# Three float32r passes for k, v and the scores of a fused attention stage, with one buffer for x's halves and the rotation of k moved ahead

## The reference

```
q = rms_norm((x @ wq) as 16 heads of 128) * q_norm_w      k = rms_norm((x @ wk) as 4 heads) * k_norm_w
v = (x @ wv) as 4 heads                                    k_ctx, v_ctx: 64 context rows per batch
q = q * cos + rotate_half(q) * sin                         k likewise; k_ctx is not rotated
scores = q . [k_ctx, k] / sqrt(128) + causal mask          probs = softmax(scores)
out = (probs @ [v_ctx, v]) @ wo                            x = x + tanh(g) * out
```

## Time and profile before

| | us |
|---|---|
| median of 3 runs (range) | 2099.92 (2099.11 to 2105.03) |
| the profiled execution, its own time | 2102.94 |
| its span, first to last instruction | 2101.2 |
| first score of slot 0 / end of the stage's last product, from the span's start | 55.92 / 1154.9 |

### The profile page before, as it was taken

The page is one execution under the profiler, slowest core; times in us unless marked ns, Lnnn a source line. Parts: engine busy times, 40 slices in busy tenths (PEclk is TensorE's granted clock), DMA queues, the critical chain, the costliest instruction groups (busy, mean ns, idle before and its releaser), DMA issues. The chain is left out here.

```text
span 2101.2 us, 27108 instructions
## 1 busy us (share of the span) xinstructions
PE 1903.4 (91%) x9540; PEld 1345.5 (64%) x9540; DVE 1112.5 (53%) x2265; ACT 1043.9 (50%) x2245; POOL 962.2 (46%) x862
## 2 busy tenths in 40 slices
PE   6899999999999999999998899999999768849998
PEld 4566766666666666666665777768999546624443
DVE  3444543456455664456443548624434468747886
ACT  2455555544454445444443321115665266647775
POOL 3544554344544444444441100007888336537774
PEclk8999999999999999999999799999999979979999
DMA  7111111211112111111000410036889580000000
GB/s 232 42 47 47 46 32 43 61 29 47 32 32 66 47 47 33 31 46 47 7 0 7 153 51 21 21 123 175 237 242 255 121 191 1 1 0 16 21 21 26
DMA packets 114005, 141.67 MB, mean 67 GB/s; under 512 B 37440, under 2 KB 69184, under 8 KB 113680
## 3 DMA queue, kind: packets, MB, share of 16 engines
q1 hardware_dynamic: 106704, 123.16, 19.1%
q0 software_dynamic: 7168, 16.78, 3.8%
HBM read 105.31 MB, written 29.36 MB: 64 GB/s over the span
## 5 line engine op out<-in xcount | busy, mean ns | idle before, releaser
L680 POOL TENSOR_TENSOR a_xcl<-xT,a_xch 128x512 fp32r<-128x512 f32 x64 | 82.4, 1288 | 406.5 <-ACT a_xch L510 406.5
L832 PE MATMUL a_A<-a_pT,a_vf 128*128 128x512 f32 (+1 forms) x448 | 239.8, 617 | 1.4 <-ACT a_pT L526 1.2
L597 DVE TENSOR_REDUCE a_nmax<-a_S 128x1 f32<-128x192 f32 (+3 forms) x256 | 138.6, 553 | 183.6 <-PE a_S L781 183.5
L780 PE MATMUL a_S<-a_kT,a_qT 128*128 128x288 f32 (+3 forms) x640 | 213.7, 432 | 2.2 <-ACT a_pr_odd L516 2.2
L120 PE MATMUL a_A<-a_wlo,a_xch 128*128 128x512 f32 x256 | 152.4, 595 | 32.1 <-DVE a_qb L643 26.5
L516 ACT ACTIVATE a_pr_odd<-a_S,a_nmax 128x320 f32<-128x320 f32 (+1 forms) x128 | 81.1, 635 | 180.4 <-DVE a_nmax L597 179.2
L526 ACT ACTIVATE a_pT<-a_TR 128x512 f32<-128x512 f32 (+1 forms) x224 | 133.4, 596 | 57.9 <-PE a_TR L822 57.7
L780 PEld LDWEIGHTS a_S<-a_kT,a_qT 128*128 128x128 f32 x640 | 121.3, 192 | 55.8 <-issue 24.8
L516 ACT ACTIVATE a_pr_even<-a_S,a_nmax 128x192 f32<-128x192 f32 (+1 forms) x128 | 67.2, 527 | 162.1 <-DVE a_nmax L597 162.0
L801 PE MATMUL a_A<-a_wkv,xT 128*128 128x256 f32 x512 | 136.9, 391 | 5.9 <-DVE a_qT L593 5.9
L1427 POOL TENSOR_TENSOR e_wlo<-expert_raw,e_whi 128x1408 fp32r<-128x1408 f32 x32 | 102.5, 3224 | 67.8 <-ACT e_whi L1500 67.8
(11 more groups left out here) (372 smaller groups left out, 5073.4 us busy)
## 6 DMA issues: line engine op xcount, KB each, us to landing
a_pw<-in_L_ffn_w_dram SPq DMA_DIRECT2D x96, 256.0 KB, 2.8
expert_raw<-in_L_ffn_w_gate_dram SPq DMA_DIRECT2D x16, 704.0 KB
expert_raw<-in_L_ffn_w_up_dram SPq DMA_DIRECT2D x16, 704.0 KB
expert_raw<-in_L_ffn_w_down_dram SPq DMA_DIRECT2D x16, 512.0 KB
tern<-a_tern SPq DMA_DIRECT2D x48, 128.0 KB, 1.7
x_res<-in_x_dram SPq DMA_DIRECT2D x4, 1024.0 KB, 8.8
a_raw<-in_L_xattn_wq_dram SPq DMA_DIRECT2D x4, 1024.0 KB, 5.6
a_raw<-in_L_xattn_wo_dram SPq DMA_DIRECT2D x4, 1024.0 KB, 5.4
```

What stands on the lines that cost most here:

```text
L597: ve.tensor_reduce(nmax[:, s % 2, i:i + 1], pair(s, i), AX.X, ALU.max, negate=True).then_inc(s_max, 1)
L680: pool.tensor_tensor(xcl[:, t % 2], xT[:, :, tok(t)], xch[:, t % 2].bitcast(F32), ALU.subtract).then_inc(xlo_ready, 1)
L780: pe.matmul(bank[:, lo:hi], qT[:, t % 2, hq], kT[:, par(t), lo:hi], start=True, stop=hi < nk)
L832: last = pe.matmul(A[:, A_USE["V", t, 0][0]], vf[r, par(t), i], pT[r, i % 2], start=i == 0, stop=i == nkt - 1)
```

## The change

k and v, and the scores, go through `mm3`. For that q and k are kept as halves after the transposition (`qTh`, `qTl`, `kTh`, `kTl`): ACT copies the high part from the bank, and DVE subtracts it from the bank (new letters l0, l1), which releases the bank and lets S0 go. The q halves have one buffer. The context keys land in `kcs`, and ACT and DVE split them once a batch (y). wk and wv land in `pw` and are split into `wkvh`, `wkvl` by ACT and POOL (u) in slot 13 of a group (DVE at the start); two pieces of the ternary weights are fetched later for that (`HELD`). x's halves have one buffer, those of tile s+2 are made in slot s, and k0 now waits for them. `qb` has two buffers. DVE's rotation of k (v) stands ahead of the third head's maximum, and both ternary pieces stand between N2 and M3. The wo halves are made at the end of slot 1 of a group. In POOL's order for the third tile, x now stands behind q. The tables of cosines and sines are loaded once.

```diff
-                -2: "k0 k1 H0 q0 q1 q2 q3 H1",
-                -1: "k0 k1 G0 R K T q0 q1 q2 q3 G1",
-                0: "S0 W0 W1 S1 W2 W3 P0 k0 S2 R k1 P1 V0 q0 P2 V1 S3 P3 K V2 q1 T P4 V3 q2 V4 q3",
-                1: "S0 W0 W1 S1 W2 W3 P0 k0 S2 R k1 P1 V0 S3 K q0 T V1 q1 q2 q3",
-                2: "S0 W0 W1 S1 W2 W3 P0 k0 S2 R k1 P1 V0 q0 S3 P2 V1 K q1 T V2 q2 q3",
-                3: "S0 W0 W1 S1 W2 W3 P0 k0 S2 R k1 P1 V0 q0 P2 V1 S3 P3 K V2 q1 T V3 q2 q3"}
+                -2: "k0 k1 q0 q1 H0 q2 q3 H1",
+                -1: "G0 k0 k1 K T R q0 q1 q2 q3",
+                "first": "S0 S1 k0 k1 G1 S2 R q0 S3 q1 K T q2 q3",
+                0: "S0 W0 W1 S1 W2 W3 P0 k0 k1 S2 R P1 V0 q0 P2 V1 S3 P3 K V2 q1 T P4 V3 q2 V4 q3",
+                1: "S0 W0 W1 S1 W2 W3 P0 k0 k1 S2 R P1 V0 S3 K q0 T V1 q1 q2 q3",
+                2: "S0 W0 W1 S1 W2 W3 P0 k0 k1 S2 R P1 V0 q0 S3 P2 V1 K q1 T V2 q2 q3",
+                3: "S0 W0 W1 S1 W2 W3 P0 k0 k1 S2 R P1 V0 q0 P2 V1 S3 P3 K V2 q1 T V3 q2 q3"}
...
-                 1: "x e0 j0 e1 g0 j1 e2 v r g1 n j2 e3 k t o f",
-                 2: "w x e0 j0 e1 g0 j1 e2 v r g1 n j2 e3 g2 k t o f",
+                 1: "x e0 j0 e1 g0 j1 v u e2 r g1 n w j2 e3 k t o f",
+                 2: "w x e0 j0 e1 g0 j1 v y e2 r g1 n j2 e3 g2 k t o f",
...
-    DVE_SLOT = "M0 M1 N0 D X j0 M2 N1 v N2 j1 M3 N3 B E A"
+    DVE_SLOT = "M0 M1 N0 D X v M2 N1 N2 y j0 j1 M3 l0 N3 l1 B E A"
...
-    POOL_ORDER = {-3: "r0 r1 r2 r3 x c0", -2: "w c1 x r", -1: "x q r", 0: "w x q p0 p1 r", 1: "x q p0 p1 r", 2: "w x q p0 p1 r", 3: "x q p0 p1 r"}
+    POOL_ORDER = {-3: "r0 r1 r2 r3 x w c0", -2: "c1 r", -1: "q x r", "first": "x q p0 p1 r",
+                  0: "x q p0 p1 r", 1: "x q p0 u p1 w r", 2: "w q x p0 p1 r", 3: "x q p0 p1 r"}
...
-                    if name == "x" and live(s, 3):
-                        t = s + 3
+                    if name == "x" and (s == BEGIN or live(s, 2)):
+                        t = 0 if s == BEGIN else s + 2
                         until(pool, xhi_ready, tile, t, m)
-                        pool.tensor_tensor(xcl[:, t % 2], xT[:, :, tok(t)], xch[:, t % 2].bitcast(F32), ALU.subtract).then_inc(xlo_ready, 1)
+                        pool.tensor_tensor(xcl[:], xT[:, :, tok(t)], xch[:].bitcast(F32), ALU.subtract).then_inc(xlo_ready, 1)
...
+                    if name == "l" and live(s, 1):
+                        t = s + 1
+                        if i == 0:
+                            until(ve, kh_ready, tile, t, m)
+                            ve.tensor_tensor(kTl[:, par(t), key_cols(t)], TR[:, TR_USE["K", t, 0][0], 0:P],
+                                             kTh[:, par(t), key_cols(t)].bitcast(F32), ALU.subtract).then_inc(kl_ready, 1)
+                        else:
+                            until(ve, qh_ready, tile, t, m)
+                            ve.tensor_tensor(qTl[:], TR[:, TR_USE["T", t, 0][0]], qTh[:].bitcast(F32), ALU.subtract).then_inc(ql_ready, 1)
...
                         if i == 0:
-                            until(pe, qT_ready, tile, t, m)
-                            until(pe, kT_ready, tile, t, m)
+                            until(pe, ql_ready, tile, t, m)
+                            until(pe, kl_ready, tile, t, m)
...
-                            pe.matmul(bank[:, lo:hi], qT[:, t % 2, hq], kT[:, par(t), lo:hi], start=True, stop=hi < nk)
+                            mm3(pe, bank[:, lo:hi], qTh[:, hq], qTl[:, hq], kTh[:, par(t), lo:hi], kTl[:, par(t), lo:hi], True, hi < nk)
...
                         if i == 0:
                             bank_of_A("k", t, s, m)
-                            if t < PERIOD:
-                                pe.wait_ge(xT_ready, t + 1)
+                            until(pe, xlo_ready, tile, t, m)
                             if t % PERIOD == 0:
-                                until(pe, wkv_loaded, lambda v: 32 * (v // PERIOD + 1), t, m)
+                                pe.wait_ge(kvl_ready, t // PERIOD + 1)
...
-                            last = pe.matmul(bank, xT[:, k, tok(t)], wkv[:, k].rearrange("p a n -> p (a n)"), start=k == 0, stop=k == KD - 1)
+                            last = mm3(pe, bank, xch[:, k], xcl[:, k], wkvh[:, k], wkvl[:, k], k == 0, k == KD - 1)
```

More of the change, by code:

```diff
@@ L168, in steps @@
     def steps(order, s):
-        return [(word[0], int(word[1:] or 0)) for word in order[s if s < 0 else s % BT].split()]
+        return [(word[0], int(word[1:] or 0)) for word in order[s if s < 0 else s % BT if s > 0 else "first"].split()]
     def batch_next(s):
@@ L176, in row, with context @@
         return i if s == BEGIN else s + ahead if BT <= s + ahead < PERIOD else None
+    def context(s):
+        return 0 if s == -1 else batch_next(s) // BT if s % BT == 2 and live(batch_next(s), 0) else None
     def bank_order(firsts):
@@ L362, in load_piece, with fetch_piece @@
                 def load_piece(k):
+                    if k < 2 * PIECES and all(k - held not in (0, 1) for held in HELD.values()):
+                        fetch_piece(k)
+                def fetch_piece(k):
                     j, o = k % PIECES // FFN_PIECES, k % FFN_PIECES
-                    if k < 2 * PIECES:
-                        sp.dma_start(pw[:, k % 2], piece(j, o)).then_inc(piece_loaded[k % 2], 16)
+                    sp.dma_start(pw[:, k % 2], piece(j, o)).then_inc(piece_loaded[k % 2], 16)
                 def store_tern(n):
@@ L478, in do @@
                                        ACT.Copy).then_inc(xT_ready, 1)
+                    if name == "u" and (s == BEGIN or s % PERIOD == PERIOD - 3):
+                        t = 0 if s == BEGIN else s + 3
+                        if live(t, 0):
+                            act.wait_ge(wkv_loaded, 32 * (t // PERIOD + 1))
+                            until(act, kv_full, tile, t - 1, m)
+                            act.activation(wkvh[:], wkv.rearrange("p k a n -> p k (a n)"), ACT.Copy).then_inc(kvh_ready, 1)
                     if name == "c":
@@ L489, in do @@
                         act.activation(vc[:, i], A[:, A_USE["G", i, 0][0]], ACT.Copy).then_inc(cv_copied, 1)
-                    if name == "y":
+                    if name == "y" and context(s) is not None:
+                        n = context(s)
+                        act.wait_ge(ck_loaded, 16 * (n + 1))
+                        act.activation(kTh[:, n % 2, 0:T], kcs[:], ACT.Copy).then_inc(ch_ready, 1)
+                    if name == "m":
                         act.wait_ge(gates_loaded, 32)
                         act.activation(gates[:], graw[:].rearrange("p l s -> p (l s)"), ACT.Tanh).then_inc(gates_ready, 1)
-                    if name == "w" and s % PERIOD in (2, 14):
-                        part = 0 if s % PERIOD == 14 else 1
-                        t = s + (2, -2)[part]
+                    if name == "w" and (s == BEGIN or s % PERIOD in (1, PERIOD - 2)):
+                        part = 1 if s % PERIOD == 1 else 0
+                        t = 0 if s == BEGIN else s + (2, -1)[part]
                         if live(t, 0):
@@ L570, in do @@
                         ve.tensor_scalar(veps[:, u:u + 1], mv[:, u, 1:2], 1e-5, None, ALU.add).then_inc(x_var, 1)
+                    if name == "y" and context(s) is not None:
+                        n = context(s)
+                        ve.wait_ge(ch_ready, n + 1)
+                        ve.tensor_tensor(kTl[:, n % 2, 0:T], kcs[:], kTh[:, n % 2, 0:T].bitcast(F32), ALU.subtract).then_inc(cl_ready, 1)
+                    if name == "l" and live(s, 1):
[7 more added lines that the diff above has]
+                            ve.tensor_tensor(qTl[:], TR[:, TR_USE["T", t, 0][0]], qTh[:].bitcast(F32), ALU.subtract).then_inc(ql_ready, 1)
                     if name == "X" and row(s, 5, i) is not None:
@@ L725, in bank_of_TR @@
                     if before is not None:
-                        sem, count = {"P": (pT_ready, turn(before[2])), "T": (qT_ready, tile), "K": (kT_ready, tile),
+                        sem, count = {"P": (pT_ready, turn(before[2])), "T": (ql_ready, tile), "K": (kl_ready, tile),
                                       "Z": (ctx_copied, tile), "R": (xT_ready, tile), "H": (ck_copied, tile)}[before[0]]
```

136 lines of the change are left out of this document (80 added, 56 removed), and 9 rows, old and new, of the table ACT_ORDER.

## The result

| | before | after |
|---|---|---|
| median of the runs side by side | 2100.21 us (7 runs) | 2110.46 us (2107.69 to 2113.05 in 6) |
| ratio, 95% interval | | 1.0043 [1.0031, 1.0055] |
| the profiled execution: own time / span | 2102.94 / 2101.2 | 2110.13 / 2108.3 |
| from the span's start to the first product after the stage | 1154.9 | 1157.6 |
| from there to the end: stages that the change does not touch | 946.3 | 950.7 |

The account below looks back on a forecast made before the run. TensorE, busiest at 91%, was taken as the bound, with late answers from other engines and its clock. Credits of -104 and debits of +115 gave +11 on the median 2099.9, hence 2110 us, range 2084 to 2134.

Parts of the forecast that it names:

- rival B: Whole kernel: the terms cancel, with low-clock stretches and ternary waits both at the low side; 2100 us, chance 0.23.
- (2): Scores on TensorE: three float32r passes cost less than plain float32 for most widths, nothing at the narrowest; -25 us.
- (3): q0's waits for DVE's rotation of k go, as the rotation stands earlier and k1 is done sooner; -26 us.
- (5): Nine low-clock stretches of TensorE in slots 24 to 55 go along with the waits before them; -15 us.
- (6): Start: -10 us before slot 0 and +6 in it, the first context block coming before the tables; -4 us.
- (7): k0 waits for x's halves, which POOL makes behind q in third tiles and in the first group; +71 us.
- (8): Ternary second and third tiles: both DVE pieces ahead of M3 make TensorE wait 1.1 and 2.0 us; +19 us.
- (9): ACT makes the wo halves before e3 in slots 17, 33 and 49; +2 us (0 to 5).
- (10): New TensorE waits bring 15 low-clock stretches at 1.5 us each; +23 us (5 to 35).
- rival D: Narrow score passes of 192 columns run at the float32 rate, +42 us; 2150 us, chance 0.07.
- rival C: DVE and POOL block each other: moved ternary pieces meet POOL, twelve slots pay 0.9 us more; 2121 us, chance 0.15.
- Rival A: New waits don't lower the clock, so that +23 us shrinks to +3, below five low stretches; 2089 us, chance 0.22.

Follow-up runs that it names:

- e4: Changed kernel with k and v as one plain float32 product of the high halves instead of three float32r passes; 2131.12 us, ratio 1.0137 to the kernel before.
- e3: Changed kernel with the scores as one plain float32 product of the high halves instead of three float32r passes; 2122.58 us, ratio 1.0096 to the kernel before.
- e2: Kernel before with only k0 and k1 side by side, the rotation earlier, ternary pieces behind N2 and two `qb` buffers, no split halves; 2059.89 us.
- e5: e1 plus, before slot 0, x ahead of q on POOL and the context keys' halves ahead of q's sums on ACT and DVE; 2045.95 us.
- e1: Changed kernel with POOL making x's low halves before q's normalization in third tiles; 2054.57 us, ratio 0.9772 to the kernel before.
- e6: Changed kernel with x ahead of both the wq halves and q in the third tile, on ACT and POOL; 2044.83 us.
- e7: e1 plus the fourth head's maximum moved between the two ternary pieces on DVE; 2036.06 us, ratio 0.9692 to the kernel before.

## Why the prediction was right, and where it was not

The sign, the time (2110) and the mechanism of the largest debit were right. The sum inside the stage was not: +11 was forecast and +2.7 measured. That the median came out at +10.3 is luck for the larger part: 4.4 us lie in stages that the change does not touch, which the forecast did not have, and 2.7 come from the profiled execution of before, which was above its median; the forecast named this difference (3.0) but carried its +11 over to the median as it was. In the stage itself the outcome is nearest to rival B, in which the terms cancel. Term by term:

| term | forecast | measured | from |
|---|---|---|---|
| (1) k, v passes | -19 | -19 | e4: 0.29 a tile |
| (2) score passes | -25 | -12 | e3's time; some 25 on TensorE alone |
| (3), (5) rotation and its low clock | -41 | about -37 | e2: -42, less some 5 for k0 beside k1 |
| k0 and k1 side by side | none | about -5 | e2, below |
| (4) wo halves | -15 | -15 | waits gone from the list |
| (6) start | -4 | +5 | first score and slot 0 |
| (7) k0 waits for x | +71 | +63 | 42.0 + 21.3 in the waits |
| (8) pieces ahead of M3 | +19 | +11 | slot lengths |
| (9) wo halves on ACT | +2 | +6 | slots 17, 33, 49 |
| (10) new low-clock stretches | +23 | about +12 | slot lengths |

The measured column sums to +9; the stage shows +2.7. The terms overlap: (7) counts k0's waits whole, and a part of them is time that the cheaper scores had saved. With (2) at its 25 us on TensorE the sum is -4. So the column closes to some 7 us and no better.

(1) and (4) held. (2) had the passes right and their effect wrong. In slot 58 a head of 448 columns takes 1046.94 - 1046.32 = 0.62 us where 0.61 was forecast; by such spacings in after and in e3 the passes save TensorE some 25 us. But only half of it shortens slots: fourth tiles give 0.64 of their 0.72, second ones 0.22 of 0.40 (0.07 of the difference because W0 waits for `otl`, 7.1 us in 17 waits, 5.9 in e3), plain third tiles 0.26 and ternary third tiles nothing, since k0 and T wait there for other engines. Counted over slots whose clock is the same in both, I estimate 10 us; the rest of e3's 13.6 are low stretches that fell elsewhere (slot 18 takes 19.06 us in e3 and 17.20 in after). The forecast had taken off only 2 us for such waits. A head of 192 columns costs 883.36 - 883.04 = 0.32 us in slot 48, where 0.33 was taken, so rival D's narrow pass is out.

(3), (5): the waits for the rotation went entirely, in after as in e2, and with them three more waits of q0, in slots 14, 30 and 46, which the profile of before names "issue" (5.3 us) and the forecast's 26 left out. The forecast missed too that two k steps in a row save something of their own. e2's fourth tiles without pieces take 18.00 us instead of 18.37, of which 0.26 was a rotation wait, as here in slot 19 of before:

```profile
381.61 0.47 PE L120 MATMUL a_A<-a_wlo,a_xch 128*128 128x512 f32 x1 [0.26 <-DVE a_qb L643]
```

so 0.1 is left. Plain first and third tiles, which had no such wait, gain 0.07 to 0.13 from slot 12 on, and slots 4 and 8 lose a wait of R of 0.57 each. Over all slots I estimate some 5 us; no run sets k0 beside k1 alone.

(6) was wrong in sign: -10 before slot 0 and +6 in it were forecast, +1.4 and +3.2 measured. The forecast had k0's wait of the earlier trace rows shrink. It only moved: q0 now waits 5.35 us for DVE (27.70 in the timeline), k0 of tile 1 6.06 us for x behind q (43.04), and the first score 4.1 us for the context keys' halves, since y stands behind the sums. e5 shows the last two: with both undone the first score comes 7.6 us sooner.

(7) was right in mechanism and nearly in size. Slot 58's wait is 2.54 against 2.75 forecast, its length 17.59 against 17.5. The 8 us that are missing lie in the nine third tiles, 16 us where 25 was forecast: where S0 had waited before, k0 waits less for the same x, 2.1 us in slots 18, 26, 38, 42 and 54 and 0.5 in slots 34 and 50. e1 and e6 remove it, 56 and 66 us with the clock's part.

(8) was right in mechanism and too large: ternary second tiles take 13.94 against 13.19 plain, 0.75 of the 1.1; third tiles 18.61 against 17.59, 1.0 of the 2.0, as T's wait in slot 38 is 1.32. Part of it lay in the shade of x's wait. With that wait removed, moving the maximum ahead of the second piece is worth 19.8 us up to the stage's end in the profiles of e1 and e7, 17.3 of it in the twelve ternary second and third tiles, clock included.

(9) was too small. Slot 17, which has no ternary pieces, takes 14.63 us, 1.4 more than slot 61; slots 33 and 49 take 16.46, 2.5 more than the other ternary second tiles. The 1.4 in each of the three come with the wo halves at the end of the slot; through which engine was not tried apart. The further 1.1 in slots 33 and 49 point to rival C's mechanism, which the forecast left out of its sum and which showed in just these two slots. DVE and POOL of after in slot 33:

```profile
637.76 0.49 DVE L670 TENSOR_SCALAR a_xn<-a_pw,a_nthr 128x512 bf16<-128x512 f32 x1
638.28 0.75 DVE L674 SCALAR_TENSOR_TENSOR a_tern<-a_pw,a_thr,a_xn 128x512 bf16<-128x512 f32 x1
639.14 1.60 DVE L670 TENSOR_SCALAR a_xn<-a_pw,a_nthr 128x512 bf16<-128x512 f32 x1
640.78 1.67 DVE L674 SCALAR_TENSOR_TENSOR a_tern<-a_pw,a_thr,a_xn 128x512 bf16<-128x512 f32 x1
...
644.89 0.68 DVE L619 TENSOR_TENSOR a_qTl<-a_TR,a_qTh 128x512 fp32r<-128x512 f32 x1
```

```profile
639.18 5.61 POOL L731 TENSOR_TENSOR a_wlo<-a_raw,a_whi 128x512 fp32r<-128x512 f32 x4 [1.32 <-ACT a_whi L536]
```

The second piece's two instructions take 1.60 + 1.67 = 3.27 us beside POOL's wo halves where the first piece's took 0.49 + 0.75 = 1.24, and the score after it waits 3.11 us for `qTl` (645.63 in the timeline), where it waits 0.6 after the other ternary second tiles. In the other ternary slots the pieces met no POOL instruction for more than 0.32 us. Before the change the first piece of every ternary slot met POOL's q or p (1.63 us in the earlier trace rows); the change moved it out of the way.

(10) counted 15 new low stretches; there were 8 from slot 3 to slot 62. All three slots with a 7 us wait at k0 had one, slots 6 and 10 (5.3 us) too, but only one (slot 22) of the nine third tiles with a wait of 0.5 to 2.5 us. The other two, in slots 34 and 50, began behind S0's wait of 3.11 us for `qTl`; they lengthened nothing that shows, as k0's wait became shorter by as much. Rival A was therefore half right: its mechanism took away half of the term. It did not decide, since its limit was five. These counts are of one execution.

## What to carry to other kernels

When a value becomes an operand of the busiest engine's first product in a slot, look up in the order of its producer what stands ahead of it: here one letter ahead of another, `x` and `q`, decided between 10 us slower and 48 us faster (2054.57 against 2102.17). A single buffer turns a producer that ran a slot ahead into one on the path, so its place must be chosen anew; whether two buffers would have done as well was not tried. And filler work such as the ternary pieces goes behind the short instruction that another engine waits for, one piece at a time.

## What the runs showed of the hardware that was not expected

The granted clock did not follow the length of the wait alone. In the kernel before waits of 1.3 to 2.0 us were followed by a low stretch in 9 of some 20 cases; in the changed kernel waits of 2.1 to 2.5 us at k0, behind four transpositions, were followed by one in 1 of 7. Even the same wait differs: k0's 2.87 us in slots 14, 30 and 46 brought a low stretch in all three in e1 and in the first two in e7. What else differs, the products ahead of the wait among it, was not tried apart, and each kernel has one profile, so the cause is open.

Beside POOL's subtractions a DVE instruction with one input from SBUF was slowed as much as one with two: L670 takes 0.49 us alone and 1.60 beside them, L674 0.75 and 1.67, above. The Trainium skill ("SBUF — State Buffer", Who interferes with whom) holds that an instruction of the L670 kind can take the port pair shared with GpSimd in its faster modes, and then one blocks the other; these rows agree.

Stages with the same code took 944.3 to 950.7 us in ten profiled executions, one of each of ten kernels that differ only ahead of them. That is 0.3%, as much as many a change is worth. Whether the kernel or the single execution sets it stays open: e7's own five runs lie between 2031.3 us at a mean clock of 0.964 and 2039.51 at 0.957. A change of this size has to be read from its own stage's windows as well as from the time.
